# A decoder layer on one core: query projections moved between slots of the linear-attention stage, first queries loaded earlier, bias added in four parts

## The reference

```python
x = x + linear_attention(layernorm(x))        # 16 heads, 128 features a head
x = x + cross_attention(layernorm(x), ctx)    # softmax over 154 keys
x = x + experts(layernorm(x))                 # 8 experts, top 6, and a shared one

# linear_attention, with elu1(t) = t + 1 if t > 0 else exp(t)
qkv = x @ w_qkv;  q, k, v = split(qkv)        # 16 heads of 32
q_proj = elu1(q @ proj);  k_proj = elu1(k @ proj)
kv = sum_n k_proj[n] v[n];  k_sum = sum_n k_proj[n]
attn = (q_proj @ kv) / (q_proj @ k_sum + 1e-8)
out = attn @ w_out + b_out
```

## Time and profile before

| | us |
|---|---|
| median of three runs | 2759.19 |
| lowest, highest | 2754.16, 2759.72 |
| the profiled execution's own time | 2757.15 |
| its span, first to last instruction | 2755.2 |
| `project` in it | 0 to 439 |
| `attend_linear` in it | 439 to 813 |

### The profile page before, as it was taken

The page is one execution under the profiler, slowest core; times in us unless marked ns, Lnnn a source line. Parts: engine busy times, 40 slices in busy tenths (PEclk is TensorE's granted clock), DMA queues, the critical chain, the costliest instruction groups (busy, mean ns, idle before and its releaser), DMA issues. The chain is left out here.

```text
span 2755.2 us, 34113 instructions
## 1 busy us (share of the span) xinstructions
PE 2588.1 (94%) x12656; PEld 1950.3 (71%) x12680; DVE 1305.7 (47%) x2019; ACT 904.8 (33%) x1443; POOL 339.5 (12%) x269
## 2 busy tenths in 40 slices
PE   7999996899978999999979999999998999999999
PEld 5777873566655555555568888888886888888887
DVE  4444434776746564656453443334344433334434
ACT  4565564676633232323231212121122111211121
POOL 1344352232320111011100000000000000000000
PEclk9999996999998999899989999999999999999999
DMA  6554435555322111212140000000113000000001
GB/s 180 159 123 120 127 86 142 172 157 158 111 92 84 62 55 64 75 61 92 62 156 32 23 23 23 23 23 23 46 65 141 23 23 23 23 23 23 23 23 61
DMA packets 67772, 206.94 MB, mean 75 GB/s; under 512 B 9968, under 2 KB 11760, under 8 KB 55664
## 3 DMA queue, kind: packets, MB, share of 16 engines
q1 hardware_dynamic: 67376, 204.81, 24.2%
q0 software_dynamic: 288, 0.69, 0.1%
HBM read 122.27 MB, written 58.72 MB: 66 GB/s over the span
## 5 line engine op out<-in xcount | busy, mean ns | idle before, releaser
L1885 PE MATMUL ex_pg<-ex_x,ex_w 128*128 128x512 f32 x3840 | 886.0, 391 | 3.3 <-DVE ex_lt L1768 3.3
L1885 PEld LDWEIGHTS ex_pg<-ex_x,ex_w 128*128 128x128 f32 x3840 | 724.0, 189 | 153.6 <-issue 3.5
L1900 PE MATMUL ex_pd<-ex_w,ex_ht 128*128 128x512 f32 x1920 | 446.6, 390 | 0.0
L1834 DVE TENSOR_TENSOR ex_h<-ex_s_g,ex_pg 128x512 f32<-128x512 f32 x160 | 110.1, 688 | 649.1 <-PE ex_pg L1885 648.2
L1900 PEld LDWEIGHTS ex_pd<-ex_w,ex_ht 128*128 128x128 f32 x1920 | 360.6, 188 | 74.6
L1741 ACT ACTIVATE ex_s_g<-ex_pg 128x512 f32<-128x512 f32 x160 | 95.8, 599 | 748.7 <-PE ex_pg L1885 748.6
L1806 DVE SCALAR_TENSOR_TENSOR ex_acc<-ex_pd,ex_share,ex_acc 128x512 f32<-128x512 f32 x320 | 234.4, 748 | 90.3 <-PE ex_pd L1900 84.9
L556 PE MATMUL pr_pj<-pr_xt,pr_w 128*128 128x512 f32 x768 | 186.0, 401 | 1.6 <-DVE pr_xt L459 1.4
L367 POOL TENSOR_TENSOR pr_ks_sum<-pr_ks_sum,pr_kp 128x512 f32<-128x512 f32 x128 | 165.0, 1289 | 178.8 <-DVE pr_kp L506 165.0
L556 PEld LDWEIGHTS pr_pj<-pr_xt,pr_w 128*128 128x128 f32 x768 | 146.3, 193 | 32.3 <-DVE pr_xt L459 1.8
L1272 ACT ACTIVATE cr_ring<-cr_s_bank 128x512 f32<-128x512 f32 x160 | 95.7, 598 | 201.9 <-remote 104.2
(11 more groups left out here) (178 smaller groups left out, 2815.5 us busy)
## 6 DMA issues: line engine op xcount, KB each, us to landing
stage<-in_units SPq DMA_DIRECT2D x21, 1536.0 KB, 6.4
pr_k<-pr_kq SPq DMA_DIRECT2D x192, 128.0 KB, 2.4
li_q<-q_scratch SPq DMA_DIRECT2D x96, 256.0 KB, 4.5
q_scratch<-pr_kq SPq DMA_DIRECT2D x128, 128.0 KB, 2.3
x_scratch<-cr_x SPq DMA_DIRECT2D x16, 1024.0 KB, 4.5
pr_x<-in_x SPq DMA_DIRECT2D x8, 1024.0 KB, 5.5
li_x<-in_x SPq DMA_DIRECT2D x8, 1024.0 KB, 7.8
x_scratch<-li_x SPq DMA_DIRECT2D x8, 1024.0 KB, 3.9
```

Source lines behind the costliest of these rows:

```text
L1834: nc.vector.tensor_tensor(h[:, f], s_g[:, f], pg[2 * f + 1][:], ALU.mult).then_inc(h_set, 1)
L1885: mm = nc.tensor.matmul(pg[2 * f + which][:], w[:, slot, sp_, col:col + P], x3[:, m, k, c * TB:(c + 1) * TB], start=(n == 0), stop=(n == 3 ...
L1900: mm = nc.tensor.matmul(pd[t][:], ht[:, s % 2, sp_, f, t * P:(t + 1) * P], w[:, slot, m, WD + f * D:WD + (f + 1) * D], start=(n == 0), sto ...
```

## The change

In `attend_linear`:

- `PLAN`: XQ 2 leaves slot 2 for the start of slot 6. XQ 3 leaves the start of slot 6 and is cut: four matmuls after T 0 in slot 6, eight after ND 2 in slot 7. T 1 moves from slot 6 to slot 7, so that T 1, T 2 and T 3 end the turn. ScalarE and VectorE follow: ScalarE takes XQ 2 in slot 6 and XQ 3 in slot 7, and the halves of all four T are made at the end of slot 7 (before, two in slot 6 and two in slot 7). The two stores of XQ 2 and XQ 3 are both issued in slot 7, ahead of the load of the next block's x.
- ScalarE copies the denominators between the two heads of slot 0, not after both.
- The low half of the reciprocals goes from VectorE to GpSimd. The bias goes in as four instructions of 512 columns: tile 0, low half of reciprocal 0, tile 1, low half of reciprocal 1, then the four `norm_lo`, then tiles 2 and 3.

In `project`:

- The normalisation moves from ScalarE to VectorE, as one subtract-and-multiply. The shift on GpSimd and the negated mean on VectorE go.
- In each g, ScalarE and VectorE do two feature steps, the first finished projection, the other two feature steps, and the rest.

At the boundary: `k3` and `q3` become one buffer `qk3`. The queries of block 0 are loaded in `project`, group by group, as soon as the last features of the keys of that group are made. Only the constants are left to load at the start of `attend_linear`.

```diff
             for part in range(PARTS):
+                for g in (2 * part, 2 * part + 1):
+                    sp.wait_ge(q_out[part], 16 * Q_DMAS)
+                    sp.wait_ge(kp_full, STEPS * LAST + TT * (g + 1))
+                    load_group(sp, q_dram, 0, g, k3, q_in[g])
                 queries_out(LAST, part)
...
-                def norm(m, t):
-                    act.wait_ge(shift_set, m + 1)
-                    nc.scalar.activation(x[:, t], x[:, t], ACT.Identity, bias=shift[:, t:t + 1], scale=rstd[:, t:t + 1])\
-                        .then_inc(xn_set, 1)
...
+                        steps = [STEPS * i + n for n in range(TT * g, TT * g + TT)] if i >= 0 else []
+                        jobs = [key for key in ends(i, g) if key[1] in ("T", "Q", "K", "V")]
+                        for step in steps[:2]:
+                            feature(step)
+                        for key in jobs[:1]:
+                            take(key)
+                        for step in steps[2:]:
+                            feature(step)
+                        for key in jobs[1:]:
+                            take(key)
...
+                def norm(m, t):
+                    dve.wait_ge(rstd_set, m + 1)
+                    nc.vector.tensor_scalar(x[:, t], x[:, t], mv[:, t, 0:1], rstd[:, t:t + 1],
+                                            ALU.subtract, ALU.mult).then_inc(xn_set, 1)
...
-        2: [("R", 0), ("R", 1), ("R", 2), ("R", 3), ("XQ", 2, 0, 12)],
+        2: [("R", 0), ("R", 1), ("R", 2), ("R", 3)],
...
-        6: [("XQ", 3, 0, 12), ("T", 0), ("T", 1)],
-        7: [("ND", 2), ("T", 2), ("T", 3)],
+        6: [("XQ", 2, 0, 12), ("T", 0), ("XQ", 3, 0, 4)],
+        7: [("ND", 2), ("XQ", 3, 4, 12), ("T", 1), ("T", 2), ("T", 3)],
...
-                load_q(0, 0)
                 sp.dma_start(spread_raw.rearrange("p g n -> p (g n)"), a["spread"]).then_inc(const_in, 16)
-                for g in range(1, G):
-                    load_q(0, g)
                 sp.dma_start(bq[:], a["bqT"]).then_inc(const_in, 16)
...
-                    if behind and s in (1, 2, 3, 7):
-                        query_out(i - 1, (1, 2, 3, 7).index(s))
+                    if behind and s in (1, 2, 7):
+                        query_out(i - 1, (1, 2, 7).index(s))
+                    if i >= 1 and s == 7 and behind:
+                        query_out(i - 1, 3)
...
-                    nc.gpsimd.tensor_tensor(x[:], x[:], rows, ALU.add).then_inc(xb_set, 1)
+                    add_bias(i, 0)
+                    reciprocal_low(i, 0)
+                    add_bias(i, 1)
+                    reciprocal_low(i, 1)
                     for g in range(G):
                         pool.wait_ge(norm_hi, G * i + g + 1)
...
+                    add_bias(i, 2)
+                    add_bias(i, 3)
...
+                        if now and s == 0 and h == 1:
+                            take_den(i)
...
-                    if now and s == 6:
-                        turned(i, 0)
-                        turned(i, 1)
...
                     if now and s == 7:
-                        turned(i, 2)
-                        turned(i, 3)
+                        for t in range(TT):
+                            turned(i, t)
...
-                    if s in (6, 7) and now:
-                        turned(i, 2 * s - 12)
-                        turned(i, 2 * s - 11)
+                    if s == 7 and now:
+                        for t in range(TT):
+                            turned(i, t)
```

More of the change, by code:

```diff
@@ L425, in _ @@
-                        for key in ends(i, g):
-                            if key[1] in ("T", "Q", "K", "V"):
-                                take(key)
-                        if g == 2 and i + 2 < NBLK:
-                            for t in range(TT):
-                                norm(i + 2, t)
+                        steps = [STEPS * i + n for n in range(TT * g, TT * g + TT)] if i >= 0 else []
+                        jobs = [key for key in ends(i, g) if key[1] in ("T", "Q", "K", "V")]
@@ L484, in ks_out, with feature, take_all @@
                         last.then_inc(*((dve_read, 1) if j == HG - 1 else (sums_set, 1)))
+                def feature(step):
+                    dve.wait_ge(e_set, step + 1)
+                    nc.vector.scalar_tensor_tensor(slot(step), pk[step % KP_BANKS][:], 0.0, slot(step),
+                                                   ALU.max, ALU.add).then_inc(kp_set, 1)
+                def take_all(keys):
+                    for key in keys:
+                        if key[1] == "KV":
+                            kv_out(key[0])
+                        elif key[1] == "KS":
+                            ks_out(key[0])
+                        elif key[1] != "V":
+                            take(key)
                 dve.wait_ge(const_set, 1)
@@ L502, in _ @@
                     for g in range(G):
-                        for n in range(TT * g, TT * g + TT) if i >= 0 else ():
-                            step = STEPS * i + n
-                            dve.wait_ge(e_set, step + 1)
-                            nc.vector.scalar_tensor_tensor(slot(step), pk[step % KP_BANKS][:], 0.0, slot(step),
-                                                           ALU.max, ALU.add).then_inc(kp_set, 1)
-                        for key in ends(i, g):
-                            if key[1] == "KV":
-                                kv_out(key[0])
-                            elif key[1] == "KS":
-                                ks_out(key[0])
-                            elif key[1] != "V":
-                                take(key)
+                        steps = [STEPS * i + n for n in range(TT * g, TT * g + TT)] if i >= 0 else []
+                        first, jobs = ends(i, g)[:1], ends(i, g)[1:]
+                        for step in steps[:2]:
+                            feature(step)
+                        take_all(first)
+                        for step in steps[2:]:
+                            feature(step)
+                        take_all(jobs)
+                        if g == 2 and i + 2 < NBLK:
+                            for t in range(TT):
+                                norm(i + 2, t)
                         if g == 1 and i + 2 < NBLK:
@@ L620, in _, with attend_linear @@
                     piece(key, 0, length(key))
-def attend_linear(nc, a, NBLK, BLK, x_blk, q_dram, x1_dram, xq_dram, ident, f_w, kv_w, ks_w, half, stage):
+def attend_linear(nc, a, NBLK, BLK, x_blk, q_dram, x1_dram, xq_dram, ident, f_w, q3, q_in, kv_w, ks_w, half, stage):
     SLOTS, PER, QSLOTS, HBANKS, BANKS = 8, 2, 8, 3, 3
@@ L692, in attend_linear @@
         x_in, x1_out = sem("x_in"), sem("x1_out")
-        q_in = [sem(f"q_in{g}") for g in range(G)]
         xq_out = [sem(f"xq_out{n}") for n in range(2)]
@@ L867, in slot @@
                             normalised(i, g)
-                    if behind and s == 2:
-                        query(i - 1, 2)
                     if ahead and s in (3, 5):
@@ L872, in slot @@
                     if behind and s == 6:
[L873 to L876 removed]
+                        query(i - 1, 2)
                     if ahead and s == 7:
                         take_num(i + 1, 2)
+                    if behind and s == 7:
+                        query(i - 1, 3)
                     if now and s == 7:
[L880 to L881 removed]
+                        for t in range(TT):
+                            turned(i, t)
                 turns(slot)
```

92 lines of the change are left out of this document (44 added, 48 removed).

## The result

| | median us | runs | ratio to before, 95% interval |
|---|---|---|---|
| before | 2759.9 (2754.2 to 2763.4) | 8 | |
| after | 2771.7 (2764.6 to 2774.1) | 8 | 1.0039, 1.0025 to 1.0052 |

2771.7 lies in the predicted range, 2746 to 2775, but 12 us above the likeliest case. It is close to what the rival "clock harsh" gave, 2773. The profiled execution of the changed kernel has a span of 2766.0 us, 10.8 more than before, at a mean granted clock of 0.965 against 0.966. So the clock costs the median execution rather more than it costs in the trace.

What follows compares the result with a forecast made beforehand. TensorE was taken as the bound, so only its idle time and clock count. Terms -2.9 - 1.5 - 22.4 + 11.9 + 0.3 + 0.2 - 12.3 + 27.8 = +1.1 us gave 2760.3, stated as 2760; range 2746 to 2775.

Steps and rivals of the forecast that it cites:

- clock harsh: Rival: each new wait of 2.4 us and more brings a clock dip; +12.5 us, 2773; chance 0.24.
- Start and the waits in `project`: Moved normalisation saves 2.9 at the start, 1.5 at a tile wait, 22.4 at five V 3 waits with dips.
- The last body: End of `project`: waits of 2.0 and 0.7 us per group cost 8.4, dips 3.5; sum 11.9 us lost.
- I take two and a half, 3.5: Last body of `project`: two and a half clock dips taken, between none (0) and 5 us, costing 3.5.
- Between the stages: `project` to `attend_linear`: query wait goes, constant lands 4.5 us after issue; 12.3 us saved, between 13.6 and 5.4.
- The turns: `attend_linear`: new T 2 waits, O groups, turns 0 and 7 and dips, less small gains; 27.8 us lost.
- R in turns 1 to 6: `attend_linear`: GpSimd's new chain lets R start at 570.44 as before, so its wait changes by zero.
- The first O groups of turns 1 to 6: `attend_linear`: without XQ 2 ahead, O 0 waits for GpSimd's last `norm_lo`; 0.65 a turn, 3.9 us lost.
- three more, 5: `attend_linear`: three more clock dips than before, beside two waits of 2.4 to 2.5 us a turn; cost 5 us.
- The sign that was named for the clock: Forecast called wrong if the clock in `attend_linear` is away from 0.96 to 0.97.
- X late: Rival: load of x, behind XQ 3's store, comes 3 us later; R waits 1.5 more in seven turns; 2771, chance 0.05.
- The wait for T 0: Rival: in `project` something other than feature steps holds V 3, so 22.4 us are not won; 2782, chance 0.05.

Runs made afterwards that it cites:

- norm_only: Kernel before plus early query load and normalisation on VectorE; old step order in every `project` body, old turns: 2728.3 us, 0.9881.
- new_plan: best with the changed plan of the turns and tile 3's normalisation behind T 0's low half: 2727.9 us, 0.9880 of before.
- best: rec_pool with reciprocals rounded between heads 2 and 3, low halves ahead of the bias, group 0's multiplication ahead of head 4's features: 2708.6 us.
- t_fix: Changed kernel with VectorE's normalisation of tile 3 moved behind heads 14 and 15 and T 0's low half: 2764.1 us, 1.0015 or less: 1.0014.
- rec_pool: Changed kernel with the last `project` body's old order and old turns, keeping of the turn change only the reciprocals' part: 2724.4 us, 0.9863.
- r_fix: Changed kernel with ScalarE's reciprocal roundings between heads 2 and 3 and GpSimd's low halves ahead of the bias: 2764.7 us, 1.0015.
- longer_r: rec_pool with one more bias piece (1.26 us of GpSimd) ahead of the second low half: 2740.3 us, 0.9922 of before.
- load_only: Kernel before with only the early load of the first queries over the dead keys: 2751.3 us, 0.9960.

## Why the prediction came out as it did

**Start and the waits in `project`: right.** -26.8 measured for -26.5; the first projection starts at 18.08 us and not at 21.52, 3.4 earlier (2.9 predicted), and norm_only shows that the chain (cast behind the normalisation and the feature steps) was the right one. Of the 32 moved normalisations 27 take about 0.54 us. The other five take 1.52 to 1.54: each began 0.05 us behind a feature sum of GpSimd of 1.30 us and ended 0.3 us behind it (86.91 to 88.44 us against 86.86 to 88.16, for one). The Trainium skill's rule that a VectorE instruction in a two-port mode and one of GpSimd shut each other out for the whole instruction ("SBUF — State Buffer", "Who interferes with whom") fits these five rows. The queueing was judged harmless for the time, and rightly: no wait of TensorE for a normalised tile behind the first appears.

**The last body: the wait right, the clock too small.** The computed idle times of 2.0 and 0.7 us stand in the trace, group by group (here the third):

```profile
403.60 0.64 PE L630 MATMUL pr_p_kv<-pr_kp,pr_v 128*32 128x128 f32 x16
403.70 0.58 ACT L406 CAST pr_kq<-pr_pj 128x512 fp32r<-128x512 f32 x1 [3.26 <-PE pr_pj L584]
...
406.23 0.43 PE L630 MATMUL pr_p_kv<-pr_kp,pr_v 128*32 128x128 f32 x8 [1.99 <-DVE pr_kp L501]
...
407.37 0.43 PE L630 MATMUL pr_p_kv<-pr_kp,pr_v 128*32 128x128 f32 x8 [0.72 <-DVE pr_kp L501]
```

A group without a dip takes 8.9 us, as said (375.99 to 384.86, the first). The other three take 12.04, 10.47 and 10.48, so the clock falls behind each pair of waits, and once for twice as long. The step that failed is "I take two and a half, 3.5". Its count was too small, and its price does not follow from its own figure: two and a half at 1.64 are 4.1. The dip of before was not to be taken off either, since the 8.4 is 36 less 27.6 and the 27.6 contains it. In these terms four groups without a dip are 35.5 us for the 36 said, and the dips are 6.4 us for 3.5. Other executions differ: 40.3 to 47.1 us for the same body in the four traces above.

**Between the stages: right in kind, 1.6 short.** The bias, issued at 428.4, landed 6.1 us later where 4.5 was taken from a range of 3.2 to 11.35; VectorE starts 7.8 us behind the stage's end, not 6.2:

```profile
428.39 0.42 SPq L763 DMA_DIRECT2D li_bias<-in_b_out  x1
...
434.56 0.43 DVE L983 CAST li_spread<-li_den 128x512 fp32r<-128x512 f32 x1 [7.36 <-DMA li_bias<-in_b_out]
```

From its issue to VectorE's start lie 6.2 us here and 4.6 to 6.5 in the ten other traces with the early load in which VectorE waits for it, so 4.5 was at the low end. The load of x, 1 MB, is issued 0.5 us behind it in all of them; what makes the difference was not tried.

**The turns: the sum of the waits right, the clock too small.** T 2 waits 19.1 us in all, as derived (15, 2.5 and 1.6). R in turns 1 to 6 waits 15.0 us against 14.7, where zero was said. In turn 0 the gain of 1.0 is there (a wait of 2.83 us of a head is now 1.80), but R has a new wait of 1.9 behind it. The first O groups of turns 1 to 6, priced at 3.9, wait 0.3 in all (0.8 in each of these turns in new_plan, where R does not wait). So single terms were up to 3.6 us off, and that the sum comes out at +22.8, as predicted, is in part luck. The clock took 8.7, and "three more, 5" was the step that failed. From turn 1 to the end of the stage the clock falls eight times, once for twice as long, and before the change four times. What the step had wrong besides the count: it looked for dips at the new waits alone. Of the T 2 waits of turns 0 to 6 only two have one; the R waits of turns 1 to 6, as long as before, have five where they had three. The sign that was named for the clock, 0.96 to 0.97 in `attend_linear`, did not show the miss: from 519 to 770 us, the stretch of the earlier trace rows, it is 0.96 (0.98 before).

**The two other rivals.** X late did not happen: the first piece of the bias ends 0.5 us before GpSimd can start the first low half (597.2 against 597.71 in the turn above), and R waits 2.50. The wait for T 0 did not stay.

**Behind `attend_linear`: 2.6 where nothing was said.** The code there is the same in all kernels, and in the 13 traces it takes 1941.9 to 1949.8 us; the trace of before has the shortest. So 2.6 is within what single executions differ by. The stretch of low clock around the start of `attend_cross` is 17.1 us long, and 13.7 in the trace of before alone.

So one step failed: how much the clock takes beside the new waits (+5.8), with the landing (+1.6) and this tail (+2.6) behind it. "Clock harsh" was given a chance of 0.24. That its 2773 is so near is partly luck: it had the clock at 12.5 more than forecast, of which the trace has 5.8, and the rest of the distance is the landing, the tail and the median's place above the profiled execution. For and against its rivals the prediction set the five waits of 2.84, all with a dip, against one of 2.26 without. Its own count, three of the six R waits of 1.8 to 2.8 us in turns 1 to 6, was the nearer measure and was not used there. Even that would have fallen short: half of the T 2 waits gives about its "three more", and nothing in the trace of before shows that R's dips would rise to five. Why they did is open.

## What to carry to other kernels

An interleaving that removes a wait where TensorE has long work beside it adds one where it has none: apply it body by body, and read the last and first body on their own. When a job is moved in a rotation of banks or shared buffers, list for each job behind it which earlier reader it now waits for; here XQ 3 in slot 7 held T 0's cast, and that costs even when all else is fixed. Price a new wait of TensorE twice: the wait itself, and the lower clock behind it. Take the share of waits with a dip from a count of all waits of that length, and give it a wide range, since the dips at the waits that stay can change too. Where the removal of one wait leaves the number of dips as it was, look whether they have moved to the next wait.

## What the runs showed of the hardware

Whether the clock falls at a wait of TensorE, as counted in the turns of `attend_linear` (one execution of each kernel; a dip is counted where a stretch at the lower of the two levels begins during the wait or up to 1.5 us behind it):

| wait | kernel | with a dip |
|---|---|---|
| 0.6, turns 1 to 6 | best | 0 of 6 |
| 1.60 at T 2, turns 1 to 6 | new_plan, t_fix | 0 of 12 |
| 1.8 to 2.8 at R, turns 1 to 6 | before | 3 of 6 |
| 2.50 at R, turns 1 to 6 | rec_pool | 3 of 6 |
| 2.50 at R, turns 1 to 6 | after | 5 of 6 |
| 2.4 to 2.5 at T 2, turns 0 to 6 | after | 2 of 7 |
| 2.4 to 2.5 at T 2, turns 0 to 6 | r_fix | 6 of 7 |
| 3.73 at R, turns 1 to 6 | longer_r | 6 of 6 |

So a longer wait at the same place brings the lower clock more often, but its length does not settle it: the same 2.5 us at T 2 had a dip twice in seven and six times in seven, and the kernels differ only in how the reciprocals get ready and R waits. Whether that is chance or follows from the waits around it, one trace each can't say. In `project` the waits of 2.84 had a dip in 5 of 5 (before) and again in 5 of 5 (load_only), those of 1.23 in none (norm_only). Short waits close together were followed by the lower clock too: the pairs of some 2.0 and 0.7 us in the last body in 16 of 16 (at most 2.1 us behind the second), and at the end of turn 7, where 1.60 and some 1.6 us follow each other, in 4 of 4 (after, t_fix, r_fix, new_plan). A single wait of 1.49 us at the end of the stage in the kernels with the old plan had one in 3 of 9, so a short wait is not always safe either.

A dip costs 1.2 to 1.6 us where TensorE is the bound behind it (rec_pool: turns of 42.4 us against 41.15 without; last body of after: groups of 10.47 against 8.87). Where the clock stays low for twice as long, it costs 2.0 (longer_r: 44.4 against 41.15 + 1.23) to 3.2 us (the group of 12.04). In the changed kernel's turns one dip at R costs some 0.5 us (44.8 and 44.9 against 44.3), since R's matmuls there wait for VectorE anyway; the turn with a double one and another at T 2 took 47.7.
